# A transformer in four stages: a weight piece moved, a normalisation on ScalarE, a reordered last attention block

## The reference

```python
x = x + attn_a(layernorm(x))   # 2 heads of 64, rotary angles on half of each head, softmax, output product
x = x + ffn(layernorm(x))      # 128 -> 512 gated, two 512 x 512 layers with exact GELU, 512 -> 128
x = x + attn_b(layernorm(x))   # 16 heads of 8, causal mask, softmax
x = x + ffn(layernorm(x))      # the same weights again

def ffn(x):                    # tlin(x, w, s) = (x @ w.T) * s, w in {-1, 0, 1}
    h = silu(tlin(x, w1, s1)) * tlin(x, w2, s2)
    h = gelu(tlin(h, h1, g1)); h = gelu(tlin(h, h2, g2))
    return tlin(h, w3, s3)
```

## Time and profile before

| | us |
|---|---|
| median of 3 runs | 813.91 |
| the three runs | 818.03, 813.91, 810.95 |
| profiled execution, own time | 808.73 |
| its span on the core | 806.9 |
| mean granted TensorE clock | 0.944 |
| first attention, start to the flag's branch | about 0 to 139 |
| last block of the second attention | about 574 to 617 |

### The profile page before, as it was taken

One profiled execution on the slowest core, in us unless ns is written; L12 is line 12 of the kernel. 1 busy time (PEld: TensorE's weight loads), 2 busy tenths in 40 slices (PEclk: granted clock), 3 DMA queues, 4 the chain that ended last, 5 costly groups with the idle time before them and its releaser, 6 DMA issues.

```text
span 806.9 us, 14446 instructions
## 1 busy us (share of the span) xinstructions
PE 699.8 (87%) x4962; PEld 490.4 (61%) x4962; DVE 522.9 (65%) x979; ACT 446.1 (55%) x777; POOL 435.2 (54%) x448
## 2 busy tenths in 40 slices
PE   4499988679999999999889899888668799999996
PEld 2255555458777777665555555555445677787784
DVE  6578997574555687466687777777444766656520
ACT  2356666446556655546656556655354455666563
POOL 4433542266777776443444444444354777777673
PEclk9788999899999999999999999999586999999998
DMA  7401000000000002532565455552202000000000
GB/s 205 69 19 34 21 0 1 2 0 1 1 0 0 0 1 79 183 106 88 179 209 166 152 184 164 177 183 83 80 2 79 1 14 1 13 13 14 13 14 26
DMA packets 30728, 52.01 MB, mean 64 GB/s; under 512 B 2256, under 2 KB 7376, under 8 KB 30672
## 3 DMA queue, kind: packets, MB, share of 16 engines
q1 hardware_dynamic: 30480, 51.01, 20.1%
q10 hardware_dynamic: 192, 0.26, 0.1%
HBM read 26.88 MB, written 24.12 MB: 63 GB/s over the span
## 4 chain that ended last, share of the span: by engine, by line
PE 49%; POOL 15%; issue 14%; DVE 11%; ACT 8%; DMA 1%; ACTq 1%; POOLq 1%; DVEq 0%; SPq 0%
PE banks L202 44%; POOL f_h_lo L1083 6%; POOL f_g_lo L1090 5%; ACT b_prob L1393 4%; DVE xn L180 4%; PE banks L194 2%; DMA w_stage<-in_wF 1%; DVE a_mx L623 1%; PE banks L925 1%; POOL b_oTn L1590 1%; PE banks L430 1%; POOL rstd L189 1%; POOL b_prob L1585 1%; DVE a_prob L635 1%; DVE a_straight L608 1%
## 5 line engine op out<-in xcount | busy, mean ns | idle before, releaser
L1090 POOL TENSOR_TENSOR f_g_lo<-f_gelu,f_g_hi 128x512 fp32r<-128x512 f32 x128 | 168.2, 1318 | 66.3 <-ACT f_g_hi L991 66.2
L990 ACT ACTIVATE f_gelu<-banks,cols 128x512 f32<-128x512 f32 x128 | 88.3, 690 | 142.6 <-PE banks L202 140.9
L202 PE MATMUL banks<-f_g_hi,whi 128*128 128x512 f32 x320 | 132.9, 415 | 15.9 <-POOL f_g_lo L1090 15.9
L1393 ACT ACTIVATE b_prob<-banks 128x768 f32<-128x768 f32 x128 | 103.6, 810 | 73.4 <-PE banks L202 68.0
L1585 POOL TENSOR_SCALAR_AFFINE_SELECT b_prob<-b_prob 128x512 f32<-128x512 f32 x128 | 81.1, 637 | 115.2 <-ACT b_prob L1393 115.2
L1476 DVE TENSOR_REDUCE b_segment_max<-banks 128x6 f32<-128x768 f32 x128 | 115.9, 946 | 35.6 <-PE banks L202 35.6
L202 PE MATMUL banks<-f_g_lo,whi 128*128 128x512 f32 x320 | 128.3, 401 | 0.0
L1083 POOL TENSOR_TENSOR f_h_lo<-f_hidden,f_h_hi 128x512 fp32r<-128x512 f32 x64 | 82.8, 1294 | 66.4 <-DVE f_h_hi L1041 60.5
L202 PE MATMUL banks<-f_h_hi,whi 128*128 128x512 f32 x256 | 105.3, 411 | 2.6 <-POOL f_h_lo L1083 2.6
L202 PE MATMUL banks<-f_h_lo,whi 128*128 128x512 f32 x256 | 102.7, 401 | 0.0
L180 DVE TENSOR_SCALAR xn<-X,mv,rstd 128x128 f32 (+1 forms) x128 | 87.7, 749 | 6.2 <-POOL rstd L189 6.2
(11 more groups left out here) (121 smaller groups left out, 1076.1 us busy)
## 6 DMA issues: line engine op xcount, KB each, us to landing
f_h_hi<-b_q_dram SPq DMA_DIRECT2D x16, 512.0 KB, 3.9
f_h_lo<-b_k_dram SPq DMA_DIRECT2D x16, 512.0 KB, 4.9
b_o_dram<-b_o SPq DMA_DIRECT2D x8, 1024.0 KB, 4.6
b_q_dram<-b_q_hi SPq DMA_DIRECT2D x16, 256.0 KB, 3.0
b_k_dram<-b_k_hi SPq DMA_DIRECT2D x16, 256.0 KB, 3.0
w_stage<-in_wF SPq DMA_DIRECT2D x8, 352.0 KB, 4.6
b_q_dram<-b_q_lo SPq DMA_DIRECT2D x8, 256.0 KB, 3.0
b_k_dram<-b_k_lo SPq DMA_DIRECT2D x8, 256.0 KB, 3.0
```

The source lines that it names most:

```text
L202: return nc.tensor.matmul(out, lhsT, rhs, start=start, stop=stop)
L990: nc.scalar.activation(gf[c % 2][:, :], z_bank[c % 2], ACT.Gelu, scale=scale).then_inc(s_gf, 1)
L1090: nc.gpsimd.tensor_tensor(lo[:, c, :], gf[c % 2][:, :], hi[:, c, :].bitcast(F32), ALU.subtract).then_inc(s_glo[c % 2], 1)
L1393: nc.scalar.activation(prob[n % 2][:, p, :, :, :], second_pass[:, :, 0:3 * P].rearrange("p b (c q) -> p c b q", c=3), ACT.Exp, scale=SCALE ...
```

## The change

In the first attention, piece 2 of the weights is handled at the end of block 0 and no longer at its front (ScalarE) or middle (VectorE, GpSimd); the second attention's constants are issued after all pieces. `xn` of blocks 2 to 7 is written by ScalarE as x * rstd + shift behind the exponentials of sequence 1; VectorE makes `shift` = -mean * rstd (128x4).

In the last block of the second attention the second half of a step gets two more banks (`second_spare`, free there), and `pe_second` waits for the exponentials of two halves back. The gate uses one pair of banks and stands in steps 2, 4, 6 and behind the block, with its low part on VectorE (`dve_hlo`). Statistics and `xn` of the second FFN's block 0 move to block 6, as does the bias of block 6; finishing of block 6 (sum, output product) moves behind the last block's steps. The second branch is gone: the whole rest of the TensorE program stands inside the first one, twice.

```diff
 class Norm:
+            def dve_shift(self, dve, b):
+                dve.wait_ge(self.rstd, b.t + 1)
+                dve.wait_ge(self.xn, TILES * b.t)
+                nc.vector.scalar_tensor_tensor(out=shift[:, :], in0=mv[:, :, 0], scalar=-1.0, in1=rstd[:, :],
+                                               op0=ALU.mult, op1=ALU.mult).then_inc(self.shift, 1)
+
+            def act_apply(self, act, b):
+                t = b.t
+                act.wait_ge(self.shift, t - 1)
+                act.wait_ge(self.read, t)
+                for s in range(TILES):
+                    nc.scalar.activation(xn[:, s, :], X[:, bass.ds(TILES * t + s, 1), :], ACT.Identity,
+                                         bias=shift[:, s:s + 1], scale=rstd[:, s:s + 1]).then_inc(self.xn, 1)
...
 first attention, sp_program (and the SyncE program at the end)
                 sp.dma_start(X[:, 2 * TILES:, :], x_dram[:, 2 * TILES:, :]).then_inc(s_x2, 16)
-                sp_b_constants(sp)
...
             ffn["sp_split"](sp)
+            sp_b_constants(sp)
...
 first attention, act_body
-                if two:
+                if two and not is_block(b, 0):
                     ffn["beside"]["act"](act, n2)
...
                 act_exp(act, b, 1)
+                if two:
+                    norm.act_apply(act, n2)
                 act_normalise(act, b, 1)
...
+                if is_block(b, 0):
+                    ffn["beside"]["act"](act, n2)
...
 first attention, dve_body (pool_body moves its piece behind pool_rope(n2, 0) in the same way)
                 if two:
-                    norm.dve_apply(dve, n2, False)
+                    norm.dve_shift(dve, n2)
...
+                if two and not is_block(b, 0):
+                    ffn["beside"]["dve"](dve, n2)
                 if two:
-                    ffn["beside"]["dve"](dve, n2)
                     dve_rope(dve, n2, "q")
                     dve_rope(dve, n2, "qr")
+                if is_block(b, 0):
+                    ffn["beside"]["dve"](dve, n2)
...
 feed-forward: pe_gate, act_tanh, dve_gate take a pair of banks; new dve_hlo
-            def pe_gate(pe, n, c, parts):
+            def pe_gate(pe, n, c, parts, pair=None):
+                slot = c % 2 if pair is None else pair
...
-                if c >= 2:
+                if pair is not None and c:
+                    pe.wait_ge(s_hf[(c - 1) % 2], 2 * t + (c - 1) // 2 + 1)
+                elif c >= 2:
...
+            def dve_hlo(dve, n, c):
+                dve.wait_ge(s_hhi, KC * n.t + c + 1)
+                nc.vector.tensor_tensor(hlo[n.odd][:, c, :], hf[c % 2][:, :], hhi[n.odd][:, c, :].bitcast(F32),
+                                        ALU.subtract).then_inc(s_hlo[c % 2], 1)
...
 second attention
+            second_spare = banks5[:, 1:3, :]
...
-            GATE_AT = 2
+            GATE_AT = {2: 0, 4: 1, 6: 2}
+            HEAD_PAIR = 1
...
+            def second_banks(b, p):
+                return second_spare if p and is_block(b, LAST) else second_pass
...
-                wait(pe, s_ex, UNITS * b.t + PAIRS * n + p)
+                if is_block(b, LAST):
+                    if (n, p) == (0, 1):
+                        pe.wait_ge(s_red, UNITS * BLOCKS)
+                    pe.wait_ge(s_ex, UNITS * b.t + max(PAIRS * n + p - 1, 0))
+                else:
+                    wait(pe, s_ex, UNITS * b.t + PAIRS * n + p)
...
 pe_step
-                if not one and GATE_AT <= n < GATE_AT + KC:
-                    pe.wait_ge(s_red, UNITS * BLOCKS)
-                    nxt["pe_gate"](pe, FIRST_BLOCK, n - GATE_AT, parts)
...
+                if not one and n in GATE_AT:
+                    nxt["pe_gate"](pe, FIRST_BLOCK, GATE_AT[n], parts, HEAD_PAIR)
...
             def pe_last(pe, parts):
-                for n in range(GATE_AT, STEPS):
-                    pe_step(pe, LAST_BLOCK, n, True, False, False, parts)
-                pe_values(pe, LAST_BLOCK, STEPS - 1)
+                nxt = link["next"]
+                pe_body(pe, LAST_BLOCK, True, False, False, parts)
+                nxt["pe_gate"](pe, FIRST_BLOCK, KC - 1, parts, HEAD_PAIR)
+                pe.wait_ge(nxt["split_written"], 1)
+                pe_out(pe, LAST_BLOCK.after(-1))
+                pe.wait_ge(s_done, LAST)
+                nxt["pe_T"](pe, SECOND_BLOCK)
...
 dve_body
-                    if not one and n == 0:
+                    if one and not two and n == OUT_AT:
                         nxt["norm"].dve_stats(dve, FIRST_BLOCK)
+                    if one and not two and n == STEPS - 1:
                         norm.dve_free(dve)
                         nxt["norm"].dve_apply(dve, FIRST_BLOCK, True)
...
+                    if not one and n in GATE_AT:
+                        nxt["dve_gate"](dve, FIRST_BLOCK, GATE_AT[n], HEAD_PAIR)
+                        nxt["dve_hlo"](dve, FIRST_BLOCK, GATE_AT[n])
...
                 if not one:
+                    nxt["norm"].dve_apply(dve, SECOND_BLOCK, False)
+                    dve_down(dve, b.after(-1))
+                    nxt["dve_gate"](dve, FIRST_BLOCK, KC - 1, HEAD_PAIR)
+                    nxt["dve_hlo"](dve, FIRST_BLOCK, KC - 1)
                     nxt["dve_xlo"](dve, SECOND_BLOCK)
...
 pool_body
-                    if not one and n == 0:
+                    if one and not two and n == OUT_AT:
                         nxt["norm"].pool(pool, FIRST_BLOCK)
+                    if one and not two and n == STEPS - 1:
+                        pool_bias(pool, b)
                     pool_mask(pool, b, n, 1)
-                    if not one and n == T_AT:
+                    if not one and n == 3:
                         nxt["norm"].pool(pool, SECOND_BLOCK)
-                    if not one and GATE_AT <= n < GATE_AT + KC:
-                        nxt["pool_hlo"](pool, FIRST_BLOCK, n - GATE_AT)
...
 sp_out
+                if is_block(b, LAST):
+                    sp.wait_ge(s_ol, 32 * LAST)
...
 TensorE program: pe_either(pe, from_first_attention) now holds it all
                 attention_second["pe_begin"](pe, parts)
-
-            def from_second_attention(parts):
+                attention_second["pe"](pe)
                 attention_second["pe_last"](pe, parts)
                 ffn_second["pe_blocks"](pe, parts)
...
-            attention_second["pe"](pe)
-            pe_either(pe, from_second_attention)
```

More of the change, by code:

```diff
@@ L109, in build @@
         rstd = sb("rstd", [P, TILES])
+        shift = sb("shift", [P, TILES])
         xn = sb("xn", [P, TILES, E])
@@ L160, in __init__ @@
                 self.read = sem(f"{layer}_xn_transposed")
+                self.shift = sem(f"{layer}_ln_shift")
             def dve(self, dve, b, first):
@@ L733, in pool_body @@
                     pool_rope(pool, b.after(1), 1)
+                if two and not is_block(b, 0):
+                    ffn["beside"]["pool"](pool, b.after(2))
                 if two:
+                    pool_rope(pool, b.after(2), 0)
+                if is_block(b, 0):
                     ffn["beside"]["pool"](pool, b.after(2))
-                    pool_rope(pool, b.after(2), 0)
             def pool_program(pool):
@@ L1305, in pe_step @@
                     pe_maxT(pe, n1, 0)
+                if before and one and n == OUT_AT:
+                    pe.wait_ge(s_nm, HALVES * (b.t + 1) + 1)
+                    pe_out(pe, b.after(-1))
                 if not one and n == T_AT:
@@ L1308, in pe_step @@
                     nxt["pe_T"](pe, FIRST_BLOCK)
-                if not one and GATE_AT <= n < GATE_AT + KC:
-                    pe.wait_ge(s_red, UNITS * BLOCKS)
-                    nxt["pe_gate"](pe, FIRST_BLOCK, n - GATE_AT, parts)
-                if before and n == OUT_AT:
-                    if one:
-                        pe.wait_ge(s_nm, HALVES * (b.t + 1) + 1)
-                    else:
-                        pe.wait_ge(nxt["split_written"], 1)
-                    pe_out(pe, b.after(-1))
-                if not one and n == STEPS - 1:
-                    pe.wait_ge(s_done, LAST)
-                    nxt["pe_T"](pe, SECOND_BLOCK)
+                if not one and n in GATE_AT:
+                    nxt["pe_gate"](pe, FIRST_BLOCK, GATE_AT[n], parts, HEAD_PAIR)
             def pe_body(pe, b, before, one, two, parts=None):
@@ L1513, in dve_body @@
                         dve_v(dve, n1)
-                    if before and n == OUT_AT + 1:
+                    if one and before and n == OUT_AT + 1:
                         dve_down(dve, b.after(-1))
@@ L1604, in pool_body @@
                         norm.pool(pool, b.after(2))
-                    if not one and n == 0:
+                    if one and not two and n == OUT_AT:
                         nxt["norm"].pool(pool, FIRST_BLOCK)
+                    if one and not two and n == STEPS - 1:
+                        pool_bias(pool, b)
                     pool_mask(pool, b, n, 1)
-                    if not one and n == T_AT:
+                    if not one and n == 3:
```

(4 more changed lines are left out.)

35 lines of the change are left out of this document (17 added, 18 removed).

## The result

| | before | after |
|---|---|---|
| median of the runs, us | 812.43 (4 runs) | 785.26 (4 runs: 791.89, 780.83, 789.07, 781.44) |
| ratio of after to before | | 0.972, 95% interval 0.967 to 0.977 |
| profiled execution, us (granted clock) | 808.73 (0.944) | 791.89 (0.945) |
| ratio in a second comparison (6 against 11 runs) | | 0.975, 0.970 to 0.981 |

By the two ratios the change makes the kernel 20 to 23 us faster. The medians of the first comparison lie 27 us apart; they rest on four runs each and take in a slow run before, 818.03, which the ratios leave out. The prediction had 23.1 us of gain, a time of 790.8 and a range of 782 to 800.

A forecast was written before the change was run, and what follows sets the result against it. The prediction saw no one busiest engine but a chain of waits at handovers between engines. Gains of 6.9 + 3.2 + 13 = 23.1 us took the profiled 808.73 to 785.6, or 790.8 measured as the median runs; range 782 to 800.

The forecast's parts named there:

- Part 1: First attention's start: piece 2 at the end of block 0 brings block 1's inverse from 48.88 to 42.0, gain 6.9 us.
- its load is no cost: Piece 2's load: even landing no earlier than 35.39, it costs nothing, since ScalarE wants it only at about 38.
- Part 2: First attention's loop: xn by ScalarE, four in 1.4 us, saves 0.65 us in each of five blocks, 3.2 us.
- Part 3: Last block of the second attention: two pairs of banks and the new order gain 13 us, bounds 8 and 15.5.
- The 15.5 us: Last block at full clock: first gate product of the second FFN's block 1 at 603.7 against 619.25 before.
- A pair of steps: Last block: two steps with one gate product take 4.9 us at full clock, near 7.5 on TensorE at 1.2 GHz.
- The clock from 568 to 590: TensorE's granted clock around the last block's first half: near 0.5 there would show the prediction wrong.
- The tail chain: Last block: chunk 1, both reciprocals, GpSimd's normalising, then four masks until 596.9, TensorE idle from about 592.
- The low part on VectorE: Last block: contention with GpSimd costs chunks 1 and 3 up to 0.6 us each; part 3 would give 11.8.
- Work moved to block 6: Statistics, xn and bias in block 6 cost nothing if TensorE's remaining work covers them; uncovered some 2 us.
- The slower rival: Second attention's block 6: TensorE waits for statistics, falls to 1.2 GHz for whole blocks; 815 and above, chance 0.03.
- The clock rival: TensorE at 1.2 GHz in most of the last block and in block 1: gain 16.2, time 797.7, chance 0.22.

The follow-up runs named there:

- e1: Changed kernel with piece 2 back at the front of block 0 and the constants ahead of pieces 2 to 7: 793.3 us, ratio 0.983 to the kernel before.
- e2: Changed kernel with only the second attention's constants issued ahead of pieces 2 to 7 again: 787.5 us, ratio 0.977 to the kernel before.
- e3: Changed kernel with only piece 2 back at the front of block 0, constants still last: 787.1 us, ratio 0.978 to the kernel before.
- e5: Changed kernel with second branch, last block and block 6 as in the kernel before: 801.1 us, ratio 0.987 to the kernel before.
- e7: Changed kernel with only the last block's low part f_h_lo on GpSimd again: 793.8 us, ratio 0.981 to the kernel before.
- e6: Changed kernel with only the second pair of banks taken away in the last block: 798.1 us, ratio 0.986 to the kernel before.
- e9: Changed kernel with both reciprocals of block 6 moved ahead of gate chunk 1, into step 3: 785.4 us, ratio 0.972 to the kernel before.
- e8: Changed kernel with only the second branch put back, ahead of the whole last block: 790.0 us, ratio 0.975 to the kernel before.
- e0: The changed kernel run again, nothing altered: 785.9 us, ratio 0.975 to the kernel before.
- e10: Changed kernel with only VectorE's count of a piece done one block later, behind shift: 784.3 us, ratio 0.970 to the kernel before.

## Why the prediction was right, point by point

- *Part 1, 6.9 us:* 6.5 by the marker, 7.0 and 7.4 by e1. The inverse was at 42.41 for 42.0. The step "its load is no cost" held (e2). What the prediction did not see is that the load's place alone would have done it (e3).
- *Part 2, 3.2 us:* as a matter of order the term was a third too large. Four `xn` take 1.65 us, not 1.4, and the gain is 5 x 0.45 = 2.25 us. The line through the rows of 256 and 704 columns gave 0.38 us for 128 columns; I then took 0.35, because I thought that shorter instructions overlap more. They cost 0.41 each, above both and outside the bounds of 1.25 to 1.6 for four. The Trainium skill (ScalarE: Activation LUTs, Rules for kernel authors) gives by its budget an estimate of 1.62 us for four and 2.1 us for the part, and the trace agrees with 1.65 and 2.25.
- *What the sum left out at the start:* parts 1 and 2 together moved the first FFN's table load by 13.5 us, against 6.9 + 3.2 = 10.1 forecast and 7.0 + 2.7 measured one at a time. The rest came with the blocks of 16 us, which the kernel before had and the changed one has not. The prediction read only a block of 14.4 us, and had the clock as a danger to the gain and not as a part of it. That the total came out at the forecast although part 2 was too large and this was missing is in part luck.
- *Part 3, 13 us:* 12.0 by e5. The size was right, its make-up only in part. The 15.5 us set a block at full clock against 45.2 us that ran at 0.70, so they held a gain of clock with that of the order; at the clocks that came (0.69 to 0.80) the interval gained 8.3 to 11.2 us, 7 to 8 of them idle time of TensorE. And 1.4 us lie behind the interval, which I had not looked for. A pair of steps took 5.2 us at full clock, not 4.9. The clock from 568 to 590, which was to be near 0.5 if the prediction was wrong, was 0.66 and 0.77 in the two profiles. The tail chain came as written; the first gate product of block 1, expected near 596, was at 604.0 and 591.9 in the two profiles, with the clock. The low part on VectorE took 1.00 us beside masks and 0.69 alone, so it lost 0.3 us and not the 0.6 priced at most. The Trainium skill (GPSIMD Engine Reference, Specifications) says that instructions of VectorE with two SBUF inputs contend with GpSimd, and the trace agrees with these two numbers. On GpSimd the same work would have cost 6 us (e7), so the slowing was the small term in this choice.
- *Work moved to block 6:* the traces show no cost where TensorE is at 1.2 GHz. From the output product of block 5 to the first scores of the last block it took 7.88 us before and 7.82 after. At full clock TensorE waits 1.56 us there for a mask (in e6, e7 and e9), about the 2 us that I had priced for the case without cover; no trace shows that block at full clock without the moved work, so what it costs there stays open.
- *The slower rival* did not come: nobody fell behind in block 6. But the second attention up to its last block took 216.0 to 223.7 us in thirteen traces with the same loop (e8 has the branch in it): 216.0 to 216.2 at a mean clock of 0.97, 219.0 to 222.5 at 0.94 to 0.95, and 223.7 at 0.92. The clock rival (797.7) had a right mechanism in the wrong place: the clock moves the total of every kernel here, the one before too, and the one before more.
- *The clock's share.* The 33 runs of the kernel before taken with the experiments had a median clock of 0.943, the six of e0 0.959; a line through each set puts them 13.7 us apart at the same clock of 0.955, which is the highest that any of the 33 had. So, as an estimate, about a third of the 20 to 23 us comes with a higher mean clock. That less waiting causes it fits the traces (e6, with its waits for exponentials back, has 0.944), but no run changes the clock alone, so it stays argued.

## What to carry to other kernels

Ask of each instruction that waits what stands ready behind it on its engine: a low part of 1.3 us cost 6 because masks stood behind its wait. When two engines alternate on one buffer, a second buffer can be the condition for every other edit around it, so price the edits together. When a stretch at a lower clock is compared with a sum at full clock, part of the difference is clock: write down TensorE's idle time and its granted clock for both. And when a load is late, look first at what stands ahead of it in its queue, before the code that wants it is moved.

## What the runs showed of the hardware

- TensorE was granted 1.2 GHz in stretches in which it was busy nearly all the time (19.70 of 20 us at 0.50, above), in one execution and not in the next. The same loop took 216.0 or 223.7 us in these two.
- A branch of TensorE's program stood as 2.98 to 3.21 us of "issue" at the second branch, in the three traces that have one (before, e5, e8), and as 5.12 to 5.66 at the first, in all fourteen.
- VectorE's normalising of head 0 beside GpSimd's tensor work took 1.54 us in e3 and 2.91 in e10 in place of 0.58 for the same two instructions. Beside it stood one GpSimd instruction of 1.27 us in e3, and in e10 a `wlo` of 1.68 and one of 1.31.
